# Where the projection stands among TensorE's work in an attention slot

## The chip, the cores and the metric

One core of one Trainium2 chip runs the whole kernel in one launch. The metric is the device time of that launch in microseconds (us). The kernel before was run three times; its profiled execution is a fourth one.

## What is computed

A transformer block on 8 sequences of 512 tokens with 128 channels, all in float32:

```python
h = layernorm(x) * (1 + ca) + sa
q, k, v = h @ Wq.T, h @ Wk.T, h @ Wv.T      # 16 heads of 64
q, k = l2norm(q) * q_scale, l2norm(k) * k_scale
a = softmax(q @ k.T * 64**-0.5) @ v
x = x + ga * (a @ Wo.T + bo)
h = layernorm(x) * (1 + cb) + sb
x = x + gb * (shared_ffn(h) + routed_experts(h))   # 8 experts, 2 per token, with a capacity
```

The change lies in the attention part alone (q, k, v, scores, softmax, weighted values, output projection). The second half, router and feed-forward, is not touched.

## The kernel before

Every engine runs a program of its own in order, written out by hand, and they meet on semaphores. The attention part is a sequence of 64 **slots**, one for each unit u = 8 b + hp: b is the sequence (0 to 7, `LAST` is 7), hp the pair of heads (0 to 7). A slot has four **pairs** (`pair` 0 to 3), each for 128 query tokens and two heads. The slots are software-pipelined: while the scores of unit u are made, q, k and v of unit u+2 are projected, q and k of unit u+1 are turned round, and unit u-1 and u-2 have their probabilities turned and their values weighed.

In each pair TensorE issues, in this order (function `slot` of the tensor block):

- `project` (lines 671 to 673): three 128x384 matmuls, q, k and v of unit u+2 for 128 tokens, into bank `PJ_BANK`. They are skipped where no unit is left (sequence 7, hp 6 and 7).
- the pair's **turn**, work on the bank `XT_BANK`, which is the same bank as `M_BANK`: in pair 0 `between` (one of: output projection `project_out`, lines 760 to 762, hp 6, 7, 0 and 2; a turn of layernorm rows, line 778, hp 1 and 4; a turn of y, line 770, hp 3; the router, line 786, hp 5; in sequence 0 hp 2 and 4 a turn of shared weights instead, and nothing in hp 0, 3 and 5; nothing in hp 1 of sequence 7), in pair 1 `inverse_rows` (line 732), in pair 2 `transpose_q` (line 680), in pair 3 `transpose_k` (line 687). The turns are four 128x128 transposes.
- `scores` (line 701): six 64x512 matmuls into two of three score banks.
- `transpose_probs` (line 721): sixteen 64x64 transposes into `T`.
- `weigh_values` (line 745): four 128x512 matmuls with 64 columns of weights.

Because one bank serves all turns, each waits until the one before it has been read out. The two waits that matter here are written so:

```python
def transpose_k(w, hp):
    pe.wait_ge(qn_done, 2 * w + 2)
    pe.wait_ge(ql_done, w + 1)
...
def between(b, hp, u):
    free = (kl_done, u + 1)
```

`ql_done` is raised by VectorE's `low_q` (line 1039), `kl_done` by VectorE's `low_k` (line 1046). In its slot VectorE makes the row maxima of both score tiles of the pair first (line 1051, `row_max`), and only then `low_q` (pair 2) or `low_k` (pair 3). ScalarE's order in a pair is: copy of the projection (line 890, `copy_projection`), then `high_q` (line 899), `high_k` (line 904), the copy of the inverse rows (line 921) or the pair-0 work, then two exponentials (line 911); in pairs 1 and 3 it ends with a copy of turned probabilities (line 916). In pair 3 of hp 0 and 3 it also makes layernorm rows (line 358). GpSimd normalises q and k of unit u+1 (line 1265) before `transpose_q` may start.

Of the kernel before, what the change touches and what calls it, by code (L numbers as in the profile page):

```python
# [30 lines left out]
def after(engine, semaphore, value):  # L31

    if not (isinstance(value, int) and value <= 0):
        engine.wait_ge(semaphore, value)
# [26 lines left out]
def adaln_attention_moe(nc, x, Wq, Wk, Wv, Wo, bo, q_scale, k_scale, proj_w, proj_b, expert_bias,  # L61
# [6 lines left out]
    HP = H // 2  # L68
# [9 lines left out]
    with ExitStack() as whole:  # L78
# [212 lines left out]
        with ExitStack() as scope:  # L291
# [308 lines left out]
            def is_const(b, value):  # L600
                return isinstance(b, int) and b == value

            def units_before(b, hp):

                return HP * b + hp if isinstance(b, int) else HP

            def with_next(b, hp, ahead):

                return not (is_const(b, B) or is_const(b, LAST) and hp + ahead >= HP)
# [13 lines left out]
            def s_bank(hp, i):  # L623

                return S_BANK[(S_TILES * hp + i) % 3]
# [22 lines left out]
            with nc.Block() as block:  # L648
# [13 lines left out]
                def _(pe):  # L662
                    def project(w, hp, wb, t, front=None):

                        if front is not None or hp % HP == 0:
                            pe.wait_ge(hT_ready, NT * wb + t + 1)
                        after(pe, pj_copied, front + 1 - 7 if front is not None else NT * w + t)
                        o = (PJ_BANK if front is None else FRONT_BANKS[front])[:, 0:3 * P].rearrange("p (n c) -> p n c", n=3)
                        cols = slice(hp % HP * P, (hp % HP + 1) * P)
                        toks = slice(t * P, (t + 1) * P)  # L670
                        nc.tensor.matmul(o, hT_h[:, toks], wqkv_h[:, :, cols], start=True, stop=False)  # L671
                        nc.tensor.matmul(o, hT_h[:, toks], wqkv_l[:, :, cols], start=False, stop=False)  # L672
                        nc.tensor.matmul(o, hT_l[:, toks], wqkv_h[:, :, cols], start=False,  # L673
                                         stop=True).then_inc(pj_ready, 1)

                    def transpose_q(w, hp, free):
                        pe.wait_ge(qn_done, 2 * w + 1)
                        after(pe, *free)
                        for t in range(NT):
                            last = nc.tensor.transpose(XT_BANK[:, t * P:(t + 1) * P], qkv[:, hp % 4, t, 0:P], ident[:])  # L680
                        last.then_inc(qt_ready, 1)
# [4 lines that stand above are left out]
                        for t in range(NT):  # L686
                            last = nc.tensor.transpose(XT_BANK[:, t * P:(t + 1) * P], qkv[:, hp % 4, t, P:2 * P], ident[:])
                        last.then_inc(kt_ready, 1)

                    def scores(u, hp, pair):  # L690

                        if pair == 0:
                            pe.wait_ge(kl_done, u + 1)
                        first = S_TILES * hp + 2 * pair
                        after(pe, p_done, S_TILES * u + 2 * pair + (0 if first == 0 else -1))
                        toks = slice(pair * P, (pair + 1) * P)
                        own = parts[:, hp % 2]
                        for q, k in ((QH, KH), (QH, KL), (QL, KH)):
                            for head in range(2):
                                rows = slice(head * DH, (head + 1) * DH)  # L700
                                last = nc.tensor.matmul(s_bank(hp, 2 * pair + head)[:], own[rows, q, toks], own[rows, k],  # L701
                                                        start=((q, k) == (QH, KH)), stop=(q == QL))
                                if q == QL:
                                    last.then_inc(s_ready, 1)
# [21 lines left out]
                    def inverse_rows(u, *free):  # L726

                        pe.wait_ge(wide_done, u + 1)
                        for semaphore, value in free:
                            after(pe, semaphore, value)  # L730
                        for t in range(NT):
                            last = nc.tensor.transpose(XT_BANK[:, t * P:(t + 1) * P],
                                                       inv_wide[:, t].rearrange("p h d -> p (h d)"), ident[:])
                        last.then_inc(r_ready, 1)
# [62 lines left out]
                    def between(b, hp, u):  # L797

                        free = (kl_done, u + 1)
                        if hp in Y_HP[0:2]:  # L800
                            project_out(b, Y_HP.index(hp), free)
                            return (y_first, b + 1) if hp == Y_HP[0] else (y_more, 3 * b + 1)
                        if hp == H1T_HP and not is_const(b, LAST):
                            transpose_ln(h1_nth(b + 1), free)
                            return (h1_done, b + 2)
                        if is_const(b, 0):
                            if hp in W_HP:
                                j = W_HP.index(hp)
                                transpose_shared(j, free)
                                return (g_low, j + 1)  # L810
                            return free
                        if hp in Y_HP[2:]:
                            project_out(b - 1, Y_HP.index(hp), free)
                            return (y_more, 3 * (b - 1) + Y_HP.index(hp))
                        if hp == YT_HP:
                            transpose_y(b - 1, free)
                            return (x1_done, b)
                        if hp == H2T_HP:
                            transpose_ln(h2_nth(b - 1), free)
                            return (h2_done, b)  # L820
                        if hp == Z_HP:
                            router(b - 1, free)
                            return (z_done, b)
                        return free

                    def slot(b, hp):

                        u = HP * b + hp
                        earlier = units_before(b, hp)
                        side = (kl_done, u + 1)  # L830
                        for pair in range(NT):
                            if with_next(b, hp, 2):
                                project(u + 2, hp + 2, b + (hp + 2) // HP, pair)
                            if pair == 0:
                                side = between(b, hp, u)
                            if pair == 1 and earlier >= 1:
                                inverse_rows(u - 1, side)
                                side = (r_copied, u)
                            if pair == 2 and with_next(b, hp, 1):
                                transpose_q(u + 1, hp + 1, side)  # L840
                            if pair == 3 and with_next(b, hp, 1):
                                transpose_k(u + 1, hp + 1)
                            scores(u, hp, pair)
                            if pair < 2 and earlier >= 1:
                                transpose_probs(u - 1, pair + 2)
                            if pair >= 2:
                                transpose_probs(u, pair - 2)
                            if pair < 2 and earlier >= 2:
                                weigh_values(u - 2, hp - 2, pair + 2)
                            if pair >= 2 and u < END and earlier >= 1:  # L850
                                weigh_values(u - 1, hp - 1, pair - 2)
                            if pair >= 2 and u == END:
                                weigh_values(u - 1, hp - 1, 2 * pair - 4)
                                weigh_values(u - 1, hp - 1, 2 * pair - 3)

                    def batch(b):
                        for hp in range(HP):
                            slot(b, hp)
# [1042 lines left out]
```

## Time and profile before

| | us |
|---|---|
| three runs, median | 1296.35 (1296.24 to 1296.62) |
| profiled execution, its own time | 1295.64 |
| span of the profile | 1293.9 |
| TensorE busy | 1236.8 |
| VectorE busy | 993.2 |
| ScalarE busy | 967.5 |
| GpSimd busy | 828.7 |

The span is the time from the first to the last recorded instruction of the profiled execution; its own time has 1.7 us around it. The slots of the attention run from about 38 us to about 1000 us of the span. "PE" is TensorE's matmuls, "PEld" its weight loads, DVE is VectorE, ACT ScalarE, POOL GpSimd. A line of the timeline gives start, duration, engine, line, operation, what is written and read, and how many instructions are merged in it; the idle time ahead of it stands in brackets, with what ended it. Matmuls overlap, so a row's duration reaches into the next; the distance from start to start is what a step takes.

### The profile page before, as it was taken

How to read it: one execution, taken by the hardware profiler on the slowest of the kernel's cores; microseconds unless marked ns; L12 is line 12 of the kernel's file. 1: busy time of each engine (PE TensorE's matmuls, PEld its weight loads, DVE VectorE, ACT ScalarE, POOL GpSimd, SP SyncE). 2: the span in 40 equal slices, each digit the busy share in tenths (PEclk: the TensorE clock that was granted, in tenths of full speed). 3: DMA queues.
4: the chain of work that ended last, by engine and by line, in shares of the span. 5: the costliest groups of instructions: out<-in, count | busy, mean ns of one | idle time of the engine just before them, and what ended most of it. 6: DMA issues, size and time to landing. Idle time of an engine off the chain costs nothing. (4 is left out here: it accounts for less than half of the span.)

```text
span 1293.9 us, 28719 instructions
## 1 busy us (share of the span) xinstructions
PE 1236.8 (96%) x9690; PEld 818.5 (63%) x9690; DVE 993.2 (77%) x2048; ACT 967.5 (75%) x2066; POOL 828.7 (64%) x1652
## 2 busy tenths in 40 slices
PE   4799999999999999999999999999999598999997
PEld 4556666666666666666666666666665376788886
DVE  3678777887887887888778877887878775577766
ACT  4677778777777787877788777877787286788886
POOL 2666677767767786777677667766674085344443
PEclk8799999999999999999999999999999699899999
DMA  6000000000000000000000000000000201446451
GB/s 159 2 1 2 1 2 1 2 1 2 2 2 1 2 2 1 2 2 1 2 2 2 2 2 1 2 2 2 1 2 2 68 1 40 92 99 108 100 107 44
DMA packets 36610, 27.99 MB, mean 22 GB/s; under 512 B 8832, under 2 KB 34688, under 8 KB 36480
## 3 DMA queue, kind: packets, MB, share of 16 engines
q1 hardware_dynamic: 35296, 25.92, 9.1%
q8 instruction: 74, 1.21, 0.4%
q10 hardware_dynamic: 1184, 0.40, 0.1%
q14 instruction: 56, 0.46, 0.1%
HBM read 24.09 MB, written 2.23 MB: 20 GB/s over the span
## 5 line engine op out<-in xcount | busy, mean ns | idle before, releaser
L911 ACT ACTIVATE probs<-bank,neg_max 128x512 f32<-128x512 f32 x512 | 347.6, 684 | 212.6 <-DVE neg_max L1051 211.0
L1051 DVE TENSOR_REDUCE neg_max<-bank 128x1 f32<-128x512 f32 x512 | 329.6, 686 | 139.8 <-PE bank L701 137.7
L745 PE MATMUL bank<-probsT,qkv 128*64 128x512 f32 x1024 | 275.1, 617 | 0.3 <-DVE probsT L1211 0.3
L701 PE MATMUL bank<-operands 64*128 64x512 f32 x1536 | 248.4, 428 | 2.2 <-ACT probs L911 1.7
L721 PEld LDWEIGHTS T<-ident,probs 64*128 64x128 f32 x4080 | 167.4, 139 | 47.0 <-issue 21.4
L671 PEld LDWEIGHTS bank<-operands,hT_h 128*128 128x128 f32 x254 | 48.0, 189 | 199.0 <-issue 196.2
L721 PE MATMUL T<-ident,probs 64*128 64x64 f32 x4080 | 170.7, 223 | 2.9 <-issue 1.4
L701 PEld LDWEIGHTS bank<-operands 64*128 64x128 f32 x1536 | 125.2, 185 | 63.8 <-issue 42.3
L1255 POOL TENSOR_TENSOR sq<-qkv 128x256 f32<-128x256 f32 x252 | 150.1, 614 | 15.6 <-ACT qkv L890 15.6
L1057 DVE COPY probsT<-T 128x1024 f32<-128x1024 f32 x128 | 155.6, 1216 | 0.1
L1872 POOL TENSOR_TENSOR hid_l<-act_out,hid_h 128x512 fp32r<-128x512 f32 x64 | 82.8, 1294 | 110.8 <-ACT hid_h L1774 110.8
L1271 POOL TENSOR_TENSOR inv_wide<-inv_sum,consts 128x512 f32<-128x512 f32 x64 | 66.6, 1040 | 130.3 <-DVE inv_sum L1062 130.3
L1265 POOL TENSOR_TENSOR qkv<-qkv,rn 128x512 f32<-128x512 f32 x128 | 131.6, 1049 | 5.0
L890 ACT ACTIVATE qkv<-bank 128x384 f32<-128x384 f32 x254 | 125.2, 494 | 8.3 <-PE bank L673 4.0
L916 ACT ACTIVATE probsT<-T 128x1024 f32<-128x1024 f32 x126 | 128.7, 1022 | 0.0
L671 PE MATMUL bank<-operands,hT_h 128*128 128x384 f32 x254 | 113.2, 446 | 1.5 <-DVE hT_l L1082 1.5
L911 ACT ACTIVATION_READ_ACCUMULATOR probs<-bank,neg_max 128x1 f32 x512 | 100.3, 196 | 0.0
L1788 ACT ACTIVATE act_out<-bank,up_bias 128x512 f32<-128x512 f32 x96 | 66.3, 691 | 28.5 <-PE bank L1716 26.1
L672 PE MATMUL bank<-wqkv_l,hT_h 128*128 128x384 f32 x254 | 87.2, 343 | 0.0
L673 PE MATMUL bank<-operands,hT_l 128*128 128x384 f32 x254 | 87.0, 342 | 0.0
L1805 DVE TENSOR_TENSOR hid_l<-act_out,hid_h 128x512 fp32r<-128x512 f32 x64 | 45.7, 714 | 52.2 <-ACT hid_h L1774 52.2
L1283 POOL TENSOR_TENSOR oT_l<-oT,oT_h 128x512 fp32r<-128x512 f32 x62 | 79.2, 1277 | 4.9
(262 smaller groups left out, 2374.0 us busy)
## 6 DMA issues: line engine op xcount, KB each, us to landing
probsT<-gate_scratch SPq DMA_DIRECT2D x64, 256.0 KB, 4.8
out<-x_all SPq DMA_DIRECT2D x8, 256.0 KB, 4.9
probsT<-in_L_ffn_fc_w SPq DMA_DIRECT2D x1, 1024.0 KB, 8.2
raw<-in_L_attn_Wq SPq DMA_DIRECT2D x1, 512.0 KB, 4.7
raw<-in_L_attn_Wk SPq DMA_DIRECT2D x1, 512.0 KB, 7.5
raw<-in_L_attn_Wv SPq DMA_DIRECT2D x1, 512.0 KB, 8.7
raw_o<-in_L_attn_Wo SPq DMA_DIRECT2D x1, 512.0 KB, 8.7
route<-in_L_ffn_sh_w SPq DMA_DIRECT2D x2, 256.0 KB, 5.5
```

Source lines behind the costliest of these rows:

```text
L671: nc.tensor.matmul(o, hT_h[:, toks], wqkv_h[:, :, cols], start=True, stop=False)
L672: nc.tensor.matmul(o, hT_h[:, toks], wqkv_l[:, :, cols], start=False, stop=False)
L701: last = nc.tensor.matmul(s_bank(hp, 2 * pair + head)[:], own[rows, q, toks], own[rows, k], start=((q, k) == (QH, KH)), stop=(q == QL))
L721: last = nc.tensor.transpose(out[half][:, at:at + DH], probs[rows, (2 * pair + head) % 4, j * P:(j + 1) * P], ident[rows, rows])
L745: last = nc.tensor.matmul(O_BANK[rows, :], qkv[:, hp % 4, j, cols], probsT[:, hp % 2, head, j], start=(j == 0), stop=(j == NT - 1), skip_g ...
L890: nc.scalar.activation(qkv[:, hp % 4, t], bank[:, 0:3 * P], ACT.Copy).then_inc(pj_copied, 1)
L911: nc.scalar.activation(probs[:, i % 4], s_bank(hp, i)[:], ACT.Exp, bias=neg_max[:, i:i + 1], accum_out=row_sum[:, hp % 2, i:i + 1]).then_i ...
L916: nc.scalar.activation(pair_tiles(hp, pair), t_pair, ACT.Copy).then_inc(t_act, 1)
L1051: nc.vector.reduce_max(neg_max[:, i:i + 1], s_bank(hp, i)[:], AX.X, negate=True).then_inc(max_done, 1)
L1057: nc.vector.tensor_copy(pair_tiles(hp, pair), t_pair).then_inc(t_dve, 1)
L1255: nc.gpsimd.tensor_tensor(sq[:, t], qk, qk, ALU.mult).then_inc(sq_done, 1)
L1265: nc.gpsimd.tensor_tensor(rows, rows, by, ALU.mult).then_inc(qn_done, 1)
```

## The change

In every pair the projection of unit u+2 is issued after the turn instead of ahead of it, still ahead of the scores. Nothing is added or removed, no wait is changed, and the programs of the other engines stay as they are: ScalarE still copies the projection first and then the turned queries or keys.

```diff
--- before.py
+++ after.py
@@ -829,8 +829,6 @@
                         earlier = units_before(b, hp)
                         side = (kl_done, u + 1)
                         for pair in range(NT):
-                            if with_next(b, hp, 2):
-                                project(u + 2, hp + 2, b + (hp + 2) // HP, pair)
                             if pair == 0:
                                 side = between(b, hp, u)
                             if pair == 1 and earlier >= 1:
@@ -840,6 +838,8 @@
                                 transpose_q(u + 1, hp + 1, side)
                             if pair == 3 and with_next(b, hp, 1):
                                 transpose_k(u + 1, hp + 1)
+                            if with_next(b, hp, 2):
+                                project(u + 2, hp + 2, b + (hp + 2) // HP, pair)
                             scores(u, hp, pair)
                             if pair < 2 and earlier >= 1:
                                 transpose_probs(u - 1, pair + 2)
```

## Rows read from the trace of the kernel before

**Rows 1.** Windows: length, busy of PE, PEld, DVE, ACT, POOL; clock; DMA share; GB/s

```profile
400.00:600.00 200.00, 199.53 (x1792) 125.48 (x1791) 162.49 (x320) 155.09 (x354) 147.12 (x338) 1.00 0.01 2
```

**Rows 2.** Timeline of TensorE, pair 2 to pair 0 of the next slot

```profile
512.42 0.97 PE L701 MATMUL bank<-operands 64*128 64x512 f32 x6
...
514.82 0.44 PE L671 MATMUL bank<-operands,hT_h 128*128 128x384 f32 x1
...
515.51 0.63 PE L687 MATMUL bank<-ident,qkv 128*128 128x128 f32 x4
516.07 0.96 PE L701 MATMUL bank<-operands 64*128 64x512 f32 x6
...
518.47 0.44 PE L671 MATMUL bank<-operands,hT_h 128*128 128x384 f32 x1
...
519.10 0.46 PE L760 MATMUL bank<-oT_h,wo_h 128*128 128x512 f32 x1
...
520.67 0.96 PE L701 MATMUL bank<-operands 64*128 64x512 f32 x6
```

**Rows 3.** Timeline of VectorE, the same pairs

```profile
513.42 1.29 DVE L1051 TENSOR_REDUCE neg_max<-bank 128x1 f32<-128x512 f32 x2 [1.34 <-PE bank L701]
514.62 0.74 DVE L1039 SCALAR_TENSOR_TENSOR operands<-bank,qk_scale,operands 128x512 fp32r<-128x512 f32 x1
...
517.06 1.29 DVE L1051 TENSOR_REDUCE neg_max<-bank 128x1 f32<-128x512 f32 x2 [0.57 <-PE bank L701]
518.27 0.68 DVE L1046 TENSOR_TENSOR operands<-bank,operands 128x512 fp32r<-128x512 f32 x1
```

**Rows 4.** Timeline of ScalarE, the same pair 2

```profile
513.21 0.70 ACT L899 ACTIVATE operands<-bank,qk_scale 128x512 fp32r<-128x512 f32 x1
```

**Rows 5.** Line 687: idle time ahead of its weight loads, us, times

```profile
  issue: 15.7, 57
```

**Rows 6.** Timeline of TensorE, slot hp 6 of sequence 7, where nothing is projected

```profile
967.57 0.97 PE L701 MATMUL bank<-operands 64*128 64x512 f32 x6
...
970.62 0.47 PE L760 MATMUL bank<-oT_h,wo_h 128*128 128x512 f32 x1 [0.56 <-DVE operands L1046]
...
972.19 0.96 PE L701 MATMUL bank<-operands 64*128 64x512 f32 x6
```

**Rows 7.** Timeline of TensorE, a pair 0 without a turn

```profile
111.09 0.44 PE L671 MATMUL bank<-operands,hT_h 128*128 128x384 f32 x1
...
111.82 0.97 PE L701 MATMUL bank<-operands 64*128 64x512 f32 x6
```

**Rows 8.** Timeline of TensorE in the feed-forward: four transposes, then a matmul

```profile
1067.26 0.63 PE L1450 MATMUL T<-ident,probsT 128*128 128x128 f32 x4
1067.65 0.48 PE L1470 MATMUL bank<-operands,sh_w 128*128 128x512 f32 x1
```

**Rows 9.** Timeline, all engines, pair 2 and 3 of hp 3

```profile
333.11 0.74 DVE L1039 SCALAR_TENSOR_TENSOR operands<-bank,qk_scale,operands 128x512 fp32r<-128x512 f32 x1
...
333.66 0.44 PE L671 MATMUL bank<-operands,hT_h 128*128 128x384 f32 x1
```

**Rows 10.** Timeline, all engines, pair 2 of hp 4

```profile
344.34 2.06 POOL L1265 TENSOR_TENSOR qkv<-qkv,rn 128x512 f32<-128x512 f32 x2
...
344.78 0.44 PE L671 MATMUL bank<-operands,hT_h 128*128 128x384 f32 x1
...
345.44 0.66 PE L680 MATMUL bank<-ident,qkv 128*128 128x128 f32 x4
```

**Rows 11.** Costliest groups, last: busy, mean ns, idle ahead and its main releaser

```profile
L721 PEld LDWEIGHTS T<-ident,probs 64*128 64x128 f32 x4080 | 167.4, 139 | 47.0 <-issue 21.4
```

**Rows 12.** Windows, the same columns, near the attention's end

```profile
966.00:1000.00 34.00, 31.28 (x285) 17.41 (x285) 28.27 (x48) 24.01 (x56) 17.41 (x28) 1.00 0.01 2
```

**Rows 13.** Windows, the same columns, in the first projections, ahead of the slots

```profile
22.00:25.00 3.00, 2.96 (x9) 2.96 (x10) 1.28 (x6) 1.51 (x4) 0.00 (x0) 0.50 1.08 295
```

## The prediction

> **What bounds the kernel now.** I read the busy times by stretch first. In the middle of the attention TensorE is busy for 199.5 of 200 us, VectorE for 162, ScalarE for 155, at clock 1.00 [rows 1]. So TensorE sets the pace of the slots, and an edit of its order can cost only in one way: by a wait that was under cover and comes into the open. I looked for such waits in TensorE's timeline. Its steps are read from start to start, since matmuls overlap. I call S the start of a pair's scores and A the moment at which TensorE has the weighing of values behind it and can begin the next pair. From S to A it takes 2.40 us, as in 512.42 to 514.82 and 516.07 to 518.47 [rows 2].
>
> Next, for the two turns that wait for VectorE, I followed VectorE's timeline from the same S. **The keys' turn.** Its two row maxima start 1.00 us after S and take 1.29 us, `low_q` then runs to 515.36 [rows 3], and the keys' turn starts at 515.51 [rows 2]: 3.09 us after S, 0.69 us after A. The projection now fills 0.63 us of these 0.69 (518.47 to 519.10 shows its length where nothing waits [rows 2]), so 0.06 us of wait is already in the open. The keys' line has idle time ahead of its loads 57 times [rows 5], that is in nearly every slot: VectorE arrives just after the cover ends. **The slot's boundary.** `low_k` ends at 518.95 [rows 3], and the output projection starts at 519.10 [rows 2], just when it may. Again the projection ahead of it is the whole cover. The trace has this very place without cover: in hp 6 of sequence 7 nothing is projected, scores start at 967.57, A is 2.40 later at 969.97, and the output projection starts at 970.62, with VectorE's line 1046 named [rows 6]. That is a wait of 0.65 us.
>
> **The change, part by part.** No instruction is added or removed. In each pair three matmuls go from ahead of the turn to behind it.
>
> *What the waiting does.* TensorE issues in order, so all that is queued behind the waiting turn stands: now the projection too, then scores, turned probabilities, weighed values; behind the scores VectorE's next maxima and ScalarE's exponentials. `low_q` and `low_k` cannot come earlier in return, for they stand behind the two maxima in VectorE's queue, and those wait for the scores of their own pair. Nor later: `high_q` starts at 513.21 [rows 4] and is over before the maxima are; the projection's copy ahead of it on ScalarE starts later now, but ScalarE was not free before 512.8 anyway.
>
> *The keys' turn, 62 slots (u = 0 to 61).* Before, A to S is 1.25 us (514.82 to 516.07 [rows 2]). After: the turn still starts 0.69 after A. Four transposes inside full-array work take 0.39 us (1067.26 to 1067.65 [rows 8]), and a projection that stands directly ahead of the scores takes 0.73 us (111.09 to 111.82 [rows 7]). Sum 1.81, a loss of 0.56. In hp 3 of sequences 1 to 7 `low_q` ends at 333.85, only 0.19 after A at 333.66 [rows 9], so with the same hand-over of 0.15 the turn starts 0.34 after A: 0.34 + 0.39 + 0.73 = 1.46 against 0.63 + 0.56 = 1.19 (its turn to scores is 0.56 at most, 515.51 to 516.07 [rows 2]), a loss of 0.27. That gives 55 x 0.56 + 7 x 0.27 = 30.8 + 1.9 = 32.7 us.
>
> *The boundary, 58 slots.* These are the slots with both a pair-0 turn and a projection: 5 in sequence 0, 8 in each of sequences 1 to 6, 5 in sequence 7. In 28 of them the turn is an output projection. Before, A to S is 2.20 (518.47 to 520.67 [rows 2]). After: 0.65 wait, 1.57 for the output projection up to scores (970.62 to 972.19 [rows 6]), 0.73 for the projection, less 0.10 to 0.20, because two blocks that meet save what an exit to the scores and an entry cost (a projection takes 0.73 ahead of scores and 0.63 ahead of a turn [rows 7, 2]). I take 0.20: 2.75, a loss of 0.55. In the other 30 it is transposes or the router: 0.65 + 0.39 + 0.73 = 1.77 against 1.19 or less, a loss of about 0.60. That gives 28 x 0.55 + 30 x 0.60 = 33.4 us.
>
> *The inverse rows and the queries (pairs 1 and 2).* Order alone: 0.39 + 0.73 = 1.12 against 1.19 or less; I cost it at nothing, with 0.07 either way. The queries' turn waits for GpSimd. Its two halves take 2.06 from 344.34 on, so q is ready near 345.4, 0.6 after A at 344.78, and the turn starts at 345.44 [rows 10]: in hp 4 the projection covers this wait to the last. The other such slot is hp 1. But GpSimd's chain hangs on the pair-3 work of the slot before, and from there TensorE now comes 0.6 later (the boundary's wait), while ScalarE's layernorm rows come some 0.35 later behind the later copy. I take a net 0.3 in 13 slots, 4 us, and 1 us more for the first slots, where the clock is low.
>
> *What is given back.* The turned probabilities have idle time ahead of their loads, put down to issue, of 21.4 us in all [rows 11], part of it late copies by ScalarE and VectorE in hp 1, 3 and 4. Where TensorE comes 0.6 later, such a wait is gone. It is at most 21, and most of it is the plain cost of changing over; I take 4 us.
>
> Sum: 32.7 + 33.4 + 5 - 4 = 67 us. The profiled execution took 1295.64, so 1363; the median of the runs stands 0.7 above it: 1363.5, or 5.2%. Bounds: the loss of a place is at least 0.45 (if the projection's first load hides behind the transposes, 0.10 less) and at most the whole wait of 0.65 (nothing saved by meeting). With 120 places that is 54 to 78, with 8 given back or 8 added for queries, 46 to 86 us.
>
> One rule speaks against reading TensorE's busy time as I did. The Trainium skill (Trainium Kernel Development and Optimization, Best Practices) calls matmul busy time a bad measure of how near TensorE is to its limit, and trusts the weight loads' share more. By that share, 125 of 200 us [rows 1], TensorE would have room to take a wait in. By the rule the sum could be near 0, by rows 6 it is 67. No measure of busy time enters my sum, and the uncovered wait of 0.65 shows that the room is not where this wait is.
>
> **The rivals.**
>
> *Only one of the two places loses.* If, say, ScalarE's `high_k` or the probabilities' turns shift so that `low_k` comes early, 33 us: 1329. Against it: the wait uncovered at 970.62 [rows 6]. 0.05.
>
> *It is hidden.* Matmul ends are modelled, and TensorE may catch up behind the waits: within 2 us of 1296.35. For it: VectorE and ScalarE are idle for a fifth of the time [rows 1]. Against it: their idle time ends on scores that TensorE has not made yet, so they cannot hand anything over sooner. 0.03.
>
> *Faster.* Behind the weighed values the first full-array block now begins with the transposes' weights and not the projection's, and the saving of up to 0.05 in some 244 pairs would be 12 us: 1284. It decides only if `low_q` and `low_k` were ready by 2.40 us after S; rows 2 and 3 have them at 2.94 and 2.88 plus the hand-over. 0.03.
>
> *The clock.* With two waits in each slot the granted clock could fall to the lower of its levels, 1.2 GHz, at times. In the first projections, at clock 0.50, 9 matmuls take 3.0 us, 0.33 each [rows 13]; in the slots a whole projection with its entry takes 0.63, 0.21 each [rows 2]. If it held for one slot in eight, 8 slots of 15 us would take at least half as long again, at most twice: 1363 + 60 to 120, about 1450. Against it: 966 to 1000 us, where TensorE is idle for 8% with waits like the new ones, has clock 1.00 [rows 12]. The Trainium skill (TensorE: Matmul & The Clock Gate, A second HAM failure mode: psum-queue depth-cycling) tells of a kernel whose small idle gaps between groups of matmuls made the clock swing; the rows at 966 to 1000 do not show that here. 0.03.
>
> *Waits add up.* ScalarE now gets the projection later and then has its copy, `high_q` or `high_k` and the exponentials in one row; if that delays maxima and turned probabilities in more pairs, 0.3 more in 64 slots: 1383. 0.06.
>
> **How the numbers follow.** The forecast has 0.80. Its own bounds, 1296.35 with 46 to 86 added, are 1342 to 1382, and that is my range; it leaves out one place (0.05), hidden and faster (0.06), the clock (0.03) and most of the adding up. A difference under 0.2%, 2.6 us, could not be told from none. Faster 0.03, same 0.03, slower 0.94.
>
> **What would show it.** In a middle slot line 687 starts 3.1 us after the scores ahead of it with idle time of about 0.6 us ahead of it; line 760, 770, 778 or 786 the same behind line 1046; the projection follows each. TensorE's busy time in 200 us falls to about 185, a slot takes 16.1 us in place of 15.1, the feed-forward keeps its length, the clock stays at 1.00. I am wrong if either wait is missing, if the slots of pair 1 or 2 gain waits of their own above 0.3, or if `low_q` starts later after S than 2.2 us.

## The result and the profile after

The changed kernel takes 1349.77 us (median of 4 runs, 1348.66 to 1357.3) against 1296.35: the ratio is 1.0423 with a 95% interval of 1.0391 to 1.0455. It is slower by 53 us where 67 were forecast; 1363.5 was given, with 1342 to 1382 as the range. The profiled execution took 1348.66, its span is 1346.8, 52.9 above the span before.

The waits are where they were expected. This is the timeline of TensorE in the changed kernel, from hp 6 of sequence 3: pair 1, then the stretch that [rows 2] shows of the kernel before (pair 2, pair 3 and pair 0 of the next slot).

```profile
521.63 0.66 PE L732 MATMUL bank<-ident,inv_wide 128*128 128x128 f32 x4
522.04 0.42 PE L671 MATMUL bank<-operands,hT_h 128*128 128x384 f32 x1
...
522.75 0.96 PE L701 MATMUL bank<-operands 64*128 64x512 f32 x6
...
526.26 0.97 PE L701 MATMUL bank<-operands 64*128 64x512 f32 x6
...
529.36 0.63 PE L687 MATMUL bank<-ident,qkv 128*128 128x128 f32 x4 [0.62 <-DVE operands L1039]
529.74 0.42 PE L671 MATMUL bank<-operands,hT_h 128*128 128x384 f32 x1
...
530.44 0.96 PE L701 MATMUL bank<-operands 64*128 64x512 f32 x6
...
533.47 0.47 PE L760 MATMUL bank<-oT_h,wo_h 128*128 128x512 f32 x1 [0.57 <-DVE operands L1046]
...
534.93 0.33 PE L671 MATMUL bank<-operands,hT_h 128*128 128x384 f32 x1
...
535.55 0.97 PE L701 MATMUL bank<-operands 64*128 64x512 f32 x6
```

The keys' turn starts 3.10 us after the scores ahead of it (526.26 to 529.36), as before (3.09 [rows 2]). What changed is that nothing is done meanwhile: TensorE is idle for 0.62 us, and the projection follows. The output projection starts 3.03 us after its scores (530.44 to 533.47), with 0.57 idle. The other turns of the boundary (lines 770, 778 and 786) wait in the same way: 0.56 us is the median of each line, with line 1046 named. Here is VectorE in the same stretch, to be held against [rows 3]:

```profile
527.26 1.29 DVE L1051 TENSOR_REDUCE neg_max<-bank 128x1 f32<-128x512 f32 x2 [1.31 <-PE bank L701]
528.47 0.74 DVE L1039 SCALAR_TENSOR_TENSOR operands<-bank,qk_scale,operands 128x512 fp32r<-128x512 f32 x1
...
531.44 1.29 DVE L1051 TENSOR_REDUCE neg_max<-bank 128x1 f32<-128x512 f32 x2 [1.10 <-PE bank L701]
532.64 0.68 DVE L1046 TENSOR_TENSOR operands<-bank,operands 128x512 fp32r<-128x512 f32 x1
```

Measured from the scores it is the same to 0.01 us: maxima at 1.00, `low_q` at 2.21, `low_k` at 2.20. The next two rows are the idle time ahead of line 687 over the whole kernel (total us, times). The first is that of its weight loads, as in [rows 5]; the second is that of its matmuls, 0.65 us each.

```profile
  issue: 94.2, 64
  DVE operands L1039: 40.9, 63
```

Windows, with the columns of [rows 1], in the middle of the attention:

```profile
400.00:600.00 200.00, 183.66 (x1652) 114.86 (x1650) 150.40 (x285) 144.52 (x329) 134.65 (x296) 1.00 0.01 2
```

TensorE is busy for 183.7 of 200 us where it was 199.5, and the clock stays at 1.00 in spite of the 8% idle time. VectorE's and ScalarE's busy time in the same 200 us falls by 7% each: their work is the same, but the slots have grown.

How much of the 52.9 us lies in the attention can be read from the first and last start of a scores matmul. Line 701, before and after:

```profile
L701 PE MATMUL bank<-operands x1536: 383/394/793, 38.8 to 996.8; 64*128 64x512 f32 x192
```

```profile
L701 PE MATMUL bank<-operands x1536: 383/393/794, 39.1 to 1055.1; 64*128 64x512 f32 x192
```

The last scores start 58.3 us later. The span grew by only 52.9, so what comes behind them, the untouched feed-forward, was 5.4 us shorter. The difference is in the clock. These are windows of the stretch from 90 to 115 us behind the start of the last pair's scores, before, then after.

```profile
1086.20:1111.20 25.00, 22.77 (x81) 14.87 (x80) 9.61 (x15) 10.47 (x19) 7.88 (x9) 0.73 0.29 90
```

```profile
1144.50:1169.50 25.00, 21.89 (x102) 15.58 (x103) 12.85 (x21) 14.60 (x25) 10.37 (x11) 1.00 0.35 106
```

The program is the same there, but TensorE gets through 81 matmuls at a mean granted clock of 0.73 and through 102 at 1.00. Whether that belongs to the change was a question for the experiments.

### The profile page after: what moved, and what is told of

Its sections match the earlier page's. It is cut to its first block and busy times, and to the rows that moved or that the text cites. A ratio compares the mean times of both kernels' runs of the same rounds, so it can differ in the third digit from the quotient of the medians.

```text
span 1346.8 us, 28719 instructions
## 1 busy us (share of the span) xinstructions
PE 1212.7 (90%) x9690; PEld 802.2 (60%) x9690; DVE 988.2 (73%) x2048; ACT 967.9 (72%) x2066; POOL 829.6 (62%) x1652
## 5 line engine op out<-in xcount | busy, mean ns | idle before, releaser
L671 PE MATMUL bank<-operands,hT_h 128*128 128x384 f32 x254 | 105.9, 417 | 1.5 <-DVE hT_l L1082 1.5
L687 PEld LDWEIGHTS bank<-ident,qkv 128*128 128x128 f32 x256 | 27.1, 141 | 94.2 <-issue 94.2
```

## The experiments

For each pair of a slot the distance from scores to scores can be set against the kernel before. "By place" below means such differences, worked out from the 256 pairs of a timeline and summed over the slots of one pair or one hp. "Later" means the start of the last scores matmul against 996.8. For the changed kernel: pair 3 +30.4 us, pair 0 +30.5, pair 1 -4.5, pair 2 +1.7.

Each ratio is taken against executions of the kernel before in the same job. Their feed-forward differs by 4 to 5 us from one execution to the next (the last experiment is about that), and in the job of the keys-only, boundary-only, middle and VectorE experiments 10 of the 13 executions of the kernel before were short ones (median 1291.37). So a ratio below can be off by some 0.3%. The start of the last scores leaves the feed-forward out, but it comes from one profiled execution of each kernel.

**The keys alone.**

```diff
-                            if with_next(b, hp, 2):
+                            if with_next(b, hp, 2) and pair != 3:
                                 project(...)
...
                                 transpose_k(u + 1, hp + 1)
+                            if with_next(b, hp, 2) and pair == 3:
+                                project(...)
```

> Projection behind the turn in pair 3 only; everywhere else as before. Theory A (the cost is the wait for low_q, uncovered, 0.53 us in a slot, 0.27 in hp 3): the attention's last scores come 30 us later (pair 3 of the changed kernel holds 30.4), total 1326, or 1321 if the feed-forward part is also 5.4 us shorter as in the changed kernel. Theory B (the cost is the order itself: changing from values to transposes and from the projection to the scores costs in any pair): a quarter of 58, some 15 us: 1311. Theory C (ScalarE's later copy and high_k push the exponentials, and both places are one chain that needs both edits): near nothing, within 5 us.

Ratio 1.0262 (1.0212 to 1.0312), 1328.69 us; last scores 35.4 us later (1032.2). Pair 3 holds 31.2 of it: 0.53 in a slot, 0.26 in hp 3, as theory A has it. The order itself (B) and the chain that needs both edits (C) are out. But there are 5.7 us that A did not have, in pair 1: 0.39 in hp 1 and 0.37 in hp 4 (1.7 of it comes back in pair 2 of hp 4). The reason stands in the slot ahead. This is TensorE, from pair 3 of hp 0 (lines of this kernel's VectorE and ScalarE stand 3 further down):

```profile
300.43 0.96 PE L701 MATMUL bank<-operands 64*128 64x512 f32 x6
...
304.03 0.96 PE L701 MATMUL bank<-operands 64*128 64x512 f32 x6
305.39 0.71 PE L721 MATMUL T<-ident,probs 64*128 64x64 f32 x16 [0.40 <-issue]
```

and ScalarE:

```profile
300.54 0.49 ACT L893 ACTIVATE qkv<-bank 128x384 f32<-128x384 f32 x1 [1.11 <-PE bank L673]
...
301.41 1.64 ACT L358 ACTIVATE h_ln<-x_all,ln_shift,rstd 128x128 f32<-128x128 f32 x4
302.94 0.68 ACT L914 ACTIVATE probs<-bank,neg_max 128x512 f32<-128x512 f32 x1
...
304.27 1.02 ACT L919 ACTIVATE probsT<-T 128x1024 f32<-128x1024 f32 x1
```

ScalarE's copy of the projection now starts 0.11 us after the scores (300.43 to 300.54), for the projection is the last thing ahead of them; in the kernel before it starts 0.42 ahead of the scores at this place. In hp 0 and 3 the layernorm rows follow (0.98 after the scores, before 0.61), then two exponentials and a copy of turned probabilities, back to back; all are late together, by 0.37. The next turn of probabilities starts at 305.39, 1.36 after its scores, where it was 0.98 in the kernel before.

**The same without hp 0 and 3.**

```diff
-                            if with_next(b, hp, 2) and pair == 3:
+                            if with_next(b, hp, 2) and pair == 3 and hp not in (0, 3):
```

> The keys-only kernel without its edit in hp 0 and 3, the two slots whose pair 3 has the layernorm rows. Theory A: the 0.37 to 0.39 us that the keys-only kernel shows in pair 1 of hp 1 and hp 4 (5.3 us in all, and -1.7 given back in pair 2 of hp 4) goes, for ScalarE's row starts as before there, and with it the 7.3 us of the keys' wait in hp 0 and 3: last scores 24 us later than before (31.2 - 7.3), against 35.4. Theory G (those 0.37 come from the lengthening of slots elsewhere): pair 1 keeps its 5.3, last scores 27.5 to 28 us later.

Ratio 1.0189 (1.0159 to 1.0219), 1320.73 us; last scores 25.1 later (1021.9). Pair 1 of hp 1 and hp 4 shows 0.00. That is A's account, and G is out: the extra cost comes from the edit in those two slots. That it goes by ScalarE's full row is read from the rows above.

**The boundary alone** (the edit of the first kernel with `pair == 0`).

> Projection behind the turn in pair 0 only. Theory A: 30 us later at the attention's last scores (58 slots at about 0.52), and less in hp 1 and 4, where turned probabilities no longer wait; total 1326 or 1321. Theory B: some 15 us, 1311. Theory C: near nothing. If A holds, this run and the one with the keys alone sum to 58 to 65 us; more than 65 would mean that one wait pays part of the other in the changed kernel.

Ratio 1.0197 (1.0155 to 1.0239), 1318.63 us; last scores 23.0 later (1019.8). Pair 0 holds +31.7, 0.52 to 0.63 in a slot, A's number. 9.1 us come back elsewhere: about 0.25 each in pair 1 of hp 1 and hp 4, pair 2 of hp 4, pair 3 of hp 3 and hp 5. There the kernel before has idle time ahead of TensorE's loads: for turned probabilities (0.43 and 0.44 in pair 1 of hp 1 and hp 4, 0.52 in pair 3 of hp 3) or for `low_q` (0.43 in pair 3 of hp 5). TensorE comes later now, and that time is gone or down to 0.2. I had expected that only in part. Together with the keys alone it makes 35.4 + 23.0 = 58.4 us, within the 58 to 65 of the expectation.

**Pairs 1 and 2 alone.**

> Projection behind the turn in pairs 1 and 2 only, the two turns that do not wait for VectorE. Theory A: no wait of VectorE's; a pair is 0.04 us shorter where the turn is ready, 30 + 24 pairs or more, -4 us; but the queries' turn waits for GpSimd in the open in hp 1 and 4 with nothing given back by a longer boundary, 0.5 to 0.65 us in 13 slots, +7 us, and a few tenths in hp 3 and 5: total +2 to +9, 1298 to 1305. Theory B: +29 us, 1325. Theory C: nothing, 1296.

Ratio 1.0062 (1.0041 to 1.0082), 1301.39 us; last scores 8.0 later (1004.8). A ready turn makes its pair 0.03 to 0.05 shorter; hp 1 and hp 4 lose 0.60 each in pair 2, in the open as here in hp 1:

```profile
426.23 0.66 PE L680 MATMUL bank<-ident,qkv 128*128 128x128 f32 x4 [0.56 <-POOL qkv L1268]
```

Order alone (B), which would have cost 29 us, is out a second time. The three parts sum to 35.4 + 23.0 + 8.0 = 66.4; together they cost 58.3. By place, 5.8 of the 8.1 us lie in pairs 1 and 2 of hp 1 and hp 4. It looks as if they were paid twice when the parts stand alone, since with all three edits the boundary's wait covers ScalarE's and GpSimd's delays too; no run tests that. By the totals, executions with a like clock held against each other, the three cost about 34, 21 and 4 to 5 us, 60 in all, so how much of the 8 us is real is open.

**The cause taken away on VectorE.** The changed kernel, with the low parts between the two maxima:

```diff
                             row_max(u, hp, 2 * pair)
-                            row_max(u, hp, 2 * pair + 1)
                             if pair == 2 and with_next(b, hp, 1):
                                 low_q(u + 1, hp + 1)
                             if pair == 3 and with_next(b, hp, 1):
                                 low_k(u + 1, hp + 1)
+                            row_max(u, hp, 2 * pair + 1)
```

> The changed kernel with one edit on VectorE: low_q and low_k stand between the pair's two row maxima instead of behind both. Theory A: both are ready some 0.6 us earlier after the scores (about 2.5 us instead of 3.1), the open waits shrink from 0.65 to about 0.1, and nearly all of the loss is gone: a pair is then within 0.05 of before. The second exponential of pairs 2 and 3 comes 0.66 later, so in pair 3 the chain row sums, norms, GpSimd, queries' turn comes 0.66 later without the boundary's wait to give it back: up to 0.8 us in hp 1 and 4 and some tenths in hp 3 and 5. Total 1290 to 1315, central 1303. Theory B and C (the cost is not VectorE's queue order): 1345 or more stays.

Ratio 1.0111 (1.0068 to 1.0154), 1307.88 us; last scores 11.6 later (1008.4) in place of 58.3. TensorE, pair 2 to 3:

```profile
535.49 0.97 PE L701 MATMUL bank<-operands 64*128 64x512 f32 x6
...
538.22 0.63 PE L687 MATMUL bank<-ident,qkv 128*128 128x128 f32 x4
...
539.30 0.96 PE L701 MATMUL bank<-operands 64*128 64x512 f32 x6
```

The keys' turn starts 2.73 after the scores here, not 3.10. This slot, hp 0, is one of two (with hp 3) in which it is late; in the others the median is 2.50. The open wait for VectorE, 40.9 us in 63 places in the changed kernel, is left in two:

```profile
  DVE operands L1042: 2.7, 2
```

Pair 3 as a whole is 2.2 us under the kernel before, pair 0 1.3 under. TensorE's order is the changed one; only VectorE's place for two instructions differs, and four fifths of the loss are gone. What is left (+6.8 in pair 1, +8.5 in pair 2, nearly all in hp 1, 3, 4 and 5) was not taken apart. The second exponential of pair 2 starts 2.98 after the scores in place of 2.41, and the turned probabilities in pair 0 of hp 1, 3 and 4 start at 1.18 where 0.80 is normal; I take the rest for what hangs on that exponential, and for GpSimd's wait, which the middle pairs had alone.

**The same edit of VectorE for `low_q` alone, TensorE's order as before.**

> The kernel before with VectorE's low_q between the two maxima of pair 2; TensorE's order untouched. Theory A (in the kernel before, low_q ends 0.06 us after the projection's cover in 55 slots and 0.3 after it in hp 5): those waits go, 55 x 0.06 = 3.4 us plus up to 1.5 in hp 5: last scores 3 to 5 us earlier, a total of 3 to 5 us under the kernel before of the same job. Theory D (moving low_q up only moves the delay into the second exponential, and ScalarE passes it on to the turned probabilities): no gain or a loss of a few us.

Ratio 1.0008 (0.9996 to 1.0021), 1297.26 us: no difference in the median. The profile's last scores start 2.6 us later, and executions with a like clock are 1.2 to 1.7 us longer. The open waits of pair 3 went as A has it (-5.8 us, 0.09 in a slot, 0.31 in hp 5), but 0.39 each came up in pair 1 of hp 1 and hp 4, 0.22 and 0.45 in pair 0 of hp 5 and hp 6. In pair 0 of hp 1 the turned probabilities start 1.36 after the scores, as in the keys-only kernel, though here no projection has moved. Theory D holds there and A's sum failed: I had left out ScalarE's row.

**Selected places, twice.** In the first, the projection stands behind the turn in pair 1, in pair 2 and pair 0 of hp 0, 2, 6 and 7, and in pair 3 of all but hp 0 and 3; `low_q` always between the maxima, `low_k` in hp 1, 5, 6 and 7:

> A version put together from the measured places: projection behind the turn in pair 1 everywhere, in pair 2 of hp 0, 2, 6, 7, in pair 3 of hp 1, 2, 4, 5, 6, 7 and in pair 0 of hp 0, 2, 6, 7; low_q between the maxima everywhere, low_k between them only in pair 3 of hp 1, 5, 6, 7. Theory A with the differences by place of the kernel with both edits: pair 1 -2.3, pair 2 -1.4, pair 3 -2.9 and the 0.06 in hp 0 and 3, pair 0 -2.4: last scores some 8 to 10 us earlier, 0.7% faster than before. Theory D: the later second exponential takes it back, within 3 us of before. If a place's wait is open after all, its slots show 0.1 to 0.5 us more.

Ratio 0.9983 (0.9972 to 0.9994), 1294.8 us; last scores 1.5 us earlier, where 8 to 10 were expected. Again pair 1 of hp 1 and hp 4 lost 0.34 to 0.36, and pair 3 of hp 4 0.36. The second leaves those places alone:

```diff
-                   or (pair == 3 and hp in (1, 2, 4, 5, 6, 7)))
+                   or (pair == 3 and hp in (1, 2, 5, 6, 7)))
...
+                            early_q = pair == 2 and hp in (1, 2, 5, 6, 7) and with_next(b, hp, 1)
```

> The selected version mended by place: hp 0, 3 and 4 keep pair 3 as before, and low_q stands between the maxima only in hp 1, 2, 5, 6, 7; pairs 0, 1, 2 as in the version before this one. Theory A (what was lost there came in hp 0 and 3, where ScalarE's layernorm rows stand ahead of the exponentials and every later start of that row reaches the turned probabilities of the next slot, and in hp 4, where ScalarE keeps h2): pair 1 -2.3, pair 0 -3.4, pair 3 -3.5, pair 2 -1.3: last scores 9 to 11 us earlier than before, 0.8% faster. Theory D (a second exponential that comes later costs in any slot): -1.5 us again.

Ratio 0.9949 (0.9933 to 0.9964), 1287.02 us against 1295.98 in the same job. Those two medians flatter it, for they fall into different groups of totals; like against like it is 5.6 us (1286.16 against 1291.76, and 1290.77 against 1296.38), and the profile's last scores start 3.5 us earlier, where 9 to 11 were expected. So it is faster than both kernels, by 0.3 to 0.5%, a third to a half of what was expected. Pair 1 of hp 1 and hp 4 and pair 3 of hp 4 are back at zero or below. But pair 2 holds +3.5 us where -1.3 was expected: 0.31 came up in hp 1, and the 0.24 that hp 4 had gained is gone. 0.13 in pair 3 of hp 0 remains. The cause of either was not tried.

**The changed kernel again, for the feed-forward.**

> The changed kernel once more, unaltered, for the part behind the attention. Theory A: the last scores come again 58 us later than before (1054.5 against 996.2), whatever the total. Theory E (the feed-forward part was 5.4 us shorter by the clock's chance, not by the change): totals of both kernels fall in two groups some 5 to 8 us apart, and the kernels' difference within one group is 57 to 60 us, 4.4 to 4.6%. Theory F (the change shortens the feed-forward): its profile shows again clock 1.00 where all the others show 0.73, and the ratio stays at 1.042.

Ratio 1.0429 (1.0411 to 1.0447), 1350.74 us. Its last scores start at 1055.4, 58.6 us later than before, and this time the stretch behind the attention has the low clock:

```profile
1144.80:1169.80 25.00, 22.74 (x80) 14.89 (x80) 9.56 (x15) 10.40 (x19) 7.89 (x9) 0.73 0.30 91
```

Its span is 1352.5, 5.7 above the first profile of the same kernel. The totals fall in two groups, in both kernels: 1350.2 to 1350.7 and 1354.5 to 1355.0 here, 1291.6 to 1292.7 and 1295.7 to 1298.2 for the kernel before in this job. Between like groups the kernels differ by 58.6 and 58.5 us (medians). So theory E holds and F is out: the change costs 58.5 us, 4.5%, and the 4.2% of the first job set executions of before that had the low clock against executions of after that mostly had not.

## Why the prediction was right, and where its sizes were off

- *The mechanism* was right at every step: the two waits, at lines 687 and 760, behind lines 1039 and 1046, with idle times of 0.62 and 0.57 us where 0.6 was given; a start 3.10 after the scores where 3.1 was given; busy time of 184 in 200 us where 185 was given; the clock in the slots at 1.00. The keys-only and boundary-only kernels show each wait alone, and the edit on VectorE, by which four fifths of the loss vanish, shows what they wait for. Only the sizes of the terms were off.
- *The keys' turn*, 32.7 us predicted, 30.4 measured: a typical slot 0.53 for 0.56, hp 3 0.27 as worked out. From the turn to the scores it takes 1.08 (529.36 to 530.44) and not 1.12. Most of the difference is hp 5, counted at 0.56 and measured at 0.31: before, `low_q` starts there 2.44 after the scores and not 2.20, and the edit at the boundary alone takes 0.23 of that wait away.
- *The boundary*, 33.4 predicted, 30.5 measured: 0.50 to 0.54 in most slots, 0.63 in hp 5, where the turn is the router's. The 28 output projections were taken at 0.55 and the other 30 turns at 0.60, a sum of pieces that were each read beside an exit or an entry of their own.
- *Pairs 1 and 2 and what is given back*, +1 predicted, -2.8 measured. Each ready turn saves 0.04 (521.63 to 522.75 is 1.12, before 1.16), a gain that I had costed at nothing; hp 1 loses 0.34 to GpSimd's wait where 0.3 was taken, hp 4 only 0.10.
- *The signs of being wrong.* Two were met by a hair. The wait for GpSimd in pair 2 of hp 1 is 0.34 us longer, and a wait of its own above 0.3 in pair 1 or 2 was named as a sign; it had itself been taken at 0.3 in the sum. `low_q` starts at 2.21 and not by 2.2, but it stood at 2.20 before, so it did not move.
- So the attention's sum was 67 for 58.3. The other 5.4 us, down to 52.9, are the clock in the feed-forward, where I had said that it "keeps its length". It does, between executions with a like clock there; I had no run that showed the two groups, since the runs given of the kernel before agreed to 0.4 us.
- *The rivals.* One place only, hidden and faster are refuted, "hidden" also in the form that the prediction gives to the rule of the Trainium skill: the weight loads' share left 75 of 200 us free [rows 1], and the two waits still cost 58 us. The clock did not fall in the slots. Waits adding up, the rival with the highest chance, exists and was named with its place (ScalarE's later row), and 0.37 us of delay is measured where 0.35 had been taken; but in the changed kernel it does not show, for pair 1 of hp 1 is 0.19 shorter there. That the boundary's wait covers it is my reading.

## What to carry to other kernels

Work that stands ahead of a waiting instruction on an in-order engine is its cover; measure, from the event that starts the other engine's chain, when the wait ends and when the cover ends, and compare the two before moving anything. If they meet within a few hundredths of a microsecond, nearly the cover's whole length is the price: here 0.53 us for a cover of 0.63. The cure is in the other engine's queue, not in the waiting one's, and an edit there is paid for by whatever it pushes back: here the second exponential, whose delay costs nothing in some slots and 0.2 to 0.5 us in others (hp 1, 4, 5 and 6 with `low_q` moved alone).

## What the runs showed of the hardware

The granted clock in the feed-forward is not a property of the kernel. The same stretch, 90 to 115 us behind the last scores, had a mean granted clock of 0.73 in one profiled execution of the changed kernel and 1.00 in another. In the first it is the lower level, 0.50, for 13.7 us of the 25 and 1.00 for the rest, and the feed-forward takes 5.4 us longer. Ahead of the fall TensorE had been idle for 0.42, 0.24, 1.12 and 0.48 us, up to the router and the first biases; in the execution in which the clock did not fall the same gaps are 0.42, 0.24, 1.09 and 0.48 us. The Trainium skill (TensorE: Matmul & The Clock Gate, What's actually happening) says that the stretch over which activity is judged runs freely and is not started anew by the kernel; that the clock fell behind these gaps in one execution and not in the other agrees with it, though no run here shows the cause. A comparison that must tell 0.4% has to hold like groups against each other.
